# Router rows kept as two f16 halves, and one copy for both operands of an expert slot

## The reference

```python
x = x + y @ wo.T                                   # attention's output added
flat = _rmsnorm(x, ln2_w).reshape(-1, Cx)          # the "rows"
probs = jax.nn.softmax(flat @ router_w.T, axis=-1)
tp, ti = jax.lax.top_k(probs, TOPK)
tp = tp / (jnp.sum(tp, axis=-1, keepdims=True) + 1e-09)
weights = jnp.sum(tp[..., None] * jax.nn.one_hot(ti, NE, dtype=flat.dtype), axis=1)
for e in range(NE):
    hh = jax.nn.silu(flat @ w1[e].T) * (flat @ w3[e].T)
    out = out + weights[:, e:e + 1] * (hh @ w2[e].T)
```

## Time and profile before

| | |
|---|---|
| median of 3 runs | 642.7 us (641.38 to 644.53) |
| the profiled execution, its own time | 643.15 us |
| its span, first to last instruction | 641.2 us |
| mean granted TensorE clock | 0.911 |
| PE / DVE / ACT / POOL busy in the span | 80% / 68% / 49% / 41% |

### The profile page before, as it was taken

One profiled execution on the slowest core, in us unless ns is written; L12 is line 12 of the kernel. 1 busy time (PEld: TensorE's weight loads), 2 busy tenths in 40 slices (PEclk: granted clock), 3 DMA queues, 4 the chain that ended last, 5 costly groups with the idle time before them and its releaser, 6 DMA issues.

```text
span 641.2 us, 12049 instructions
## 1 busy us (share of the span) xinstructions
PE 512.5 (80%) x3865; PEld 285.6 (45%) x3865; DVE 438.4 (68%) x1084; ACT 316.8 (49%) x525; POOL 265.9 (41%) x300
## 2 busy tenths in 40 slices
PE   2999967799998999976767889989665766676891
PEld 2533324577776455433213323235210255466780
DVE  6898948979999556676866978997530157564653
ACT  0778976469996001202254436746522473354550
POOL 3000005035354323033536959992563037743442
PEclk9999996799999999986768999999785999799986
DMA  8999953000158500112233220011143035446775
GB/s 308 394 424 421 371 176 123 10 18 19 33 225 328 129 16 6 40 29 67 57 90 80 68 56 1 1 33 46 57 126 89 20 96 153 126 137 164 209 193 171
DMA packets 45606, 81.92 MB, mean 128 GB/s; under 512 B 8016, under 2 KB 36992, under 8 KB 41200
## 3 DMA queue, kind: packets, MB, share of 16 engines
q1 hardware_dynamic: 41824, 76.33, 36.7%
q0 software_dynamic: 2272, 4.69, 2.1%
q10 hardware_dynamic: 1456, 0.22, 0.2%
HBM read 61.72 MB, written 17.11 MB: 123 GB/s over the span
## 4 chain that ended last, share of the span: by engine, by line
PE 43%; DVE 16%; issue 8%; SPq 5%; DMA 4%; ACT 3%; another core or an unknown queue 3%; POOL 0%; ACTq 0%; DVEq 0%; POOLq 0%
PE ps L1489 8%; DVE A L2306 7%; PE ps L1666 7%; PE ps L1417 6%; PE ps L1400 5%; PE ps L1658 3%; PE ps L1566 3%; PE ps L1769 2%; SPq L770 2%; SPq L767 2%; PE ps L1514 2%; DMA A<-slots_out 2%; PE ps L1792 1%; DMA A<-slots_in 1%
## 5 line engine op out<-in xcount | busy, mean ns | idle before, releaser
L1229 ACT ACTIVATE A<-ps 128x1024 f32<-128x1024 f32 (+3 forms) x80 | 68.6, 894 | 67.1 <-PE ps L1658 47.5
L2306 DVE TENSOR_REDUCE A<-ps 128x1 f32<-128x512 f32 (+3 forms) x160 | 86.1, 603 | 12.9 <-PE ps L1566 12.2
L941 POOL TENSOR_TENSOR G<-G,A 128x1024 f32<-128x1024 f32 (+3 forms) x40 | 73.3, 1874 | 16.5 <-ACT A L1229 16.5
L1658 PE MATMUL ps<-A 97*128 97x512 f16 (+3 forms) x160 | 46.9, 379 | 17.4 <-ACT A L1229 17.4
L1566 PE MATMUL ps<-A 96*128 96x512 f16 (+3 forms) x160 | 54.6, 380 | 7.7 <-DVE A L2306 4.8
L1489 PE MATMUL ps<-A,G 128*128 128x512 f32 x128 | 60.1, 601 | 0.0
L1323 PE MATMUL ps<-R,G 128*128 128x512 f32 x128 | 59.2, 605 | 1.0 <-DVE G L1866 0.8
L1769 PE MATMUL ps<-A 128*128 128x128 f16 (+1 forms) x702 | 50.3, 228 | 7.2 <-issue 7.2
L1417 PE MATMUL ps<-R 128*128 128x128 f16 x768 | 50.4, 224 | 6.9 <-DVE x L1986 4.3
L1417 PEld LDWEIGHTS ps<-R 128*128 128x128 f16 x768 | 47.4, 101 | 14.4 <-issue 5.1
L1092 ACT ACTIVATE R<-ps,b 128x512 f32<-128x512 f32 x64 | 44.0, 687 | 16.0 <-PE ps L1400 9.5
(11 more groups left out here) (309 smaller groups left out, 939.7 us busy)
## 6 DMA issues: line engine op xcount, KB each, us to landing
A<-in_adj_t SPq DMA_DIRECT2D x16, 1024.0 KB, 17.5
A<-w_split SPq DMA_DIRECT2D x39, 341.0 KB
slots_in<-xn SPq DMA_DIRECT2D x1, 8320.0 KB, 22.4
R<-in_adj_in SPq DMA_DIRECT2D x7, 1024.0 KB, 7.2
xn<-in_adj_in SPq DMA_DIRECT2D x5, 1024.0 KB, 12.8
xT<-in_adj_in SPq DMA_DIRECT2D x4, 1024.0 KB, 13.0
A<-in_f_w SPq DMA_DIRECT2D x16, 170.5 KB
w_split<-A SPq DMA_DIRECT2D x8, 341.0 KB, 5.1
```

The costliest lines, as they stand in the source:

```text
L941: pool.tensor_tensor(total, total, probabilities(n, pair)[:, :, t0:CW], ALU.add).then_inc(s_sum, 1)
L1229: act.activation(probabilities(n, pair)[:, :, t0:CW], ps[:, 2 * pair:2 * pair + 2, t0:CW], ACT.Exp, scale=1.0 / (SQ * SQ * float(HD) ** 0. ...
L1658: last = pe.matmul(ps[:, h, t0:CW], keys(j // TPC, h // (NH // NKV))[0:KQ + 1, P * (j % TPC):P * (j % TPC) + P], queries(c, h)[0:KQ + 1, t ...
L2306: dve.reduce_max(pm[:, h, t % TPC, b:b + 1], ps[:, bank, 0:width], AX_X).then_inc(s_rmf, 1)
```

## The change

The rows are kept as two f16 halves of 128 columns in the same 512 bytes of a record. The factor `SX` goes into `rd`, so that the halves are operands as they are. The high half is written as the rows were (ACT for chunk 0, DVE for chunks 1 to 3). The low half is a new DVE operation for each tile, with `xn` and the high half as inputs; for chunk 0 it is a new unit `low_rows` in turn (2, 0). The second copy is now a copy of the first (one ACT operation for a chunk; for chunk 3 POOL as before, in f16). The transposes of a chunk become pairs of f16 products with the identity that add up in the bank, and a slot's transpose becomes two f16 products, side by side; ACT copies both at once as 256 columns, and `slot_low` on DVE is gone. What waited for DVE's low half (`s_sxl`) waits for ACT's copy (`s_sxh`).

```diff
-                       (1, 7): [("rows", 0)], (2, 1): [("tr", 0)], (2, 2): [("rows2", 0)], (2, 3): [("logit", 0)],
+                       (1, 7): [("rows", 0)], (2, 0): [("low_rows", 0)], (2, 1): [("tr", 0)], (2, 2): [("rows2", 0)], (2, 3): [("logit", 0)],
...
-            chain(pool.tensor_copy(second_rows[:, TILES[2], 0:D], first_rows[:, TILES[2], 0:D]))
+            chain(pool.tensor_copy(row_halves[1][:, TILES[2], 0:2 * D], row_halves[0][:, TILES[2], 0:2 * D]))
...
-            def router_rows(c, which):
+            def high_rows(c):
 
                 act.wait_ge(s_r2, c + 1)
...
-                    last = act.activation(row_of(which, t)[:, 0:D], xn[:, t, :], ACT.Copy, scale=rd[:, t:t + 1])
-                last.then_inc(s_fn2 if which else s_fn, 1)
+                    last = act.activation(row_halves[0][:, t, 0:D], xn[:, t, :], ACT.Copy, scale=rd[:, t:t + 1])
+                last.then_inc(s_rhi, 1)
+
+            def copy_rows(c):
+
+                act.wait_ge(s_fn, c + 1)
+                act.activation(row_halves[1][:, TPC * c:TPC * c + TPC, 0:2 * D], row_halves[0][:, TPC * c:TPC * c + TPC, 0:2 * D],
+                               ACT.Copy).then_inc(s_fn2, 1)
...
-                act.activation(x16[2 * (n % 2)], ps[:, x_bank(n), 0:P], ACT.Copy, scale=SX).then_inc(s_sxh, 1)
+                act.activation(x_pair[n % 2], ps[:, x_bank(n), 0:2 * P], ACT.Copy).then_inc(s_sxh, 1)
...
-                        last = pe.transpose(ps[:, bank, P * q:P * q + P], first_rows[:, TPC * c + q, 0:D], ident[:, :])
+                        for part in range(2):
+                            last = pe.matmul(ps[:, bank, P * q:P * q + P], row_halves[0][:, TPC * c + q, D * part:D * part + D],
+                                             ident_h[:, :], start=part == 0, stop=part == 1, skip_group_check=True)
...
-                pe.transpose(ps[:, x_bank(n), 0:P], slot_rows(n)[:, 0:D], ident[:, :]).then_inc(s_sT, 1)
+                for part in range(2):
+                    last = pe.matmul(ps[:, x_bank(n), P * part:P * part + P], slot_halves(n)[:, D * part:D * part + D], ident_h[:, :],
+                                     start=True, stop=True, skip_group_check=True)
+                last.then_inc(s_sT, 1)
...
+                if c == 0:
+                    dve.wait_ge(s_rhi, 1)
+                else:
+                    dve.wait_ge(s_r2, c + 1)
+                    for t in tiles:
+                        last = dve.tensor_scalar(row_halves[0][:, t, 0:D], xn[:, t, :], rd[:, t:t + 1], None, ALU.mult)
+                    chain(last)
+                for t in tiles:
+                    last = dve.scalar_tensor_tensor(out=row_halves[0][:, t, D:2 * D], in0=xn[:, t, :], scalar=rd[:, t:t + 1],
+                                                    in1=row_halves[0][:, t, 0:D], op0=ALU.mult, op1=ALU.subtract)
                 last.then_inc(s_fn, 1)
...
-                dve.scalar_tensor_tensor(out=x16[2 * (n % 2) + 1], in0=ps[:, x_bank(n), 0:P], scalar=SX, in1=x16[2 * (n % 2)],
-                                         op0=ALU.mult, op1=ALU.subtract).then_inc(s_sxl, 1)
```

More of the change, by code:

```diff
@@ L254, in program @@
         second_rows = R[:, NT * RW:2 * NT * RW].rearrange("p (t w) -> p t w", w=RW)
+        row_halves = [rows.rearrange("p t w -> p (t w)").bitcast(F16).rearrange("p (t w) -> p t w", w=2 * RW)
+                      for rows in (first_rows, second_rows)]
         ROWS_AT = 2 * NT * RW + 10 * NT * 8
@@ L271, in slot_rows, with slot_halves @@
             return homes[n]
+        x_pair = [A16[:, 13, 6 * CW + 2 * P * n:6 * CW + 2 * P * n + 2 * P] for n in range(2)]
+        def slot_halves(n):
+            return slot_rows(n)[:, 0:D].bitcast(F16)
         def loaded_target(n):
@@ L2332, in unit @@
                     row_statistics(what[1])
-                elif what[0] == "rows" and what[1]:
+                elif what[0] == "rows" and what[1] or what[0] == "low_rows":
                     router_rows(what[1])
@@ L2396, in router_rows @@
             def router_rows(c):
-                dve.wait_ge(s_r2, c + 1)
-                for t in range(TPC * c, TPC * c + TPC):
-                    last = dve.tensor_scalar(first_rows[:, t, 0:D], xn[:, t, :], rd[:, t:t + 1], None, ALU.mult)
+                tiles = range(TPC * c, TPC * c + TPC)
+                if c == 0:
[8 more added lines that the diff above has]
+                                                    in1=row_halves[0][:, t, 0:D], op0=ALU.mult, op1=ALU.subtract)
                 last.then_inc(s_fn, 1)
```

32 lines of the change are left out of this document (15 added, 17 removed).

## The result

The changed kernel takes 649.63 us (median of 6 runs, 647.51 to 652.17); the kernel before, on the same chip, 642.9 us. The ratio is 1.0099, with a 95% interval of 1.0062 to 1.0136: slower by more than 0.5%. The time lies 1.1 us from the forecast of 648.5 and within its range; the experiments will show that its terms were further off than that, in both directions.

What follows compares the result with a forecast made beforehand. Bound: chunk 2 without slack on PE, DVE and POOL, and SP's queue in the last 22 slots. Terms -0.4 + 0.4 + 0.9 + 4.9 = +5.8 us on 643.15 gave 649.0, forecast as 648.5 us; range 643.0 to 651.0.

Steps and rivals of the forecast that it cites:

- `low_rows` in turn (2, 0): Chunk 2: DVE's four low halves are held until POOL's block of adds runs dry, making PE late: +4.9 us.
- rival 1: Chunk 2: DVE slips in between two of POOL's adds; 643.9 to 646.4 us in all, chance 0.35.
- POOL's lateness: Chunk 2: POOL's seventh add starts 5.2 us late, but with some 3.2 us in hand it does not bind.
- Rows of chunks 1 and 2: Chunk 3, before the first scatter: eight more DVE operations start the scatter 1.85 us later; +0.9 us, between 0 and 1.85.
- Rows of chunk 3: Chunk 3's rows: four added DVE low halves (0.95), less shorter PE products (0.2) and an earlier split (0.3): net +0.4 us.
- The slots: Slots: DVE loses 11.1 us of low halves, but SP sets the late pace, so only -0.4 us (-1.0 to +0.1).
- the faster cases: Whole kernel: slots pay, or some of PE's holes in chunk 3 vanish; faster by over 0.5%, chance 0.10.
- The 1.26 us: Chunk 2: length of the one POOL add running when DVE arrives, taken as a share of the largest add's 2.38.
- Rival 2: Late slots: SP is not the bound and 22 slots gain 0.28 us each, 6.2 us; 642 to 638 us, chance 0.06.
- Rival 3: Chunk 3: holes during the scatters grow with the shift, 1.85 us or more stays; 651 us and over, chance 0.07.
- Rival 4: Slots: halves emptied by more operations than before; ruled out by the order of operations, no chance given.
- The other signs: Changed profile: PE waiting 390 to 396, POOL idle at 394, last maximum 431, scatter 1.9 us later, loads 10 us apart.

Runs made afterwards that it cites:

- e1_low_rows_earlier: Changed kernel with the first chunk's four low halves moved from turn (2, 0) to turn (1, 7): 613.68 us against 610.38 for the kernel before, ratio 1.0051.
- c_after: Changed kernel timed once more, without an edit, on the same chip as c_before: 652.8 us, ratio 1.014 to the kernel before.
- e5_odd_width: Changed kernel with turn (2, 0) as a four-column memset and four one-SBUF-input operations over 127 columns: 652.15 us against 644.07 for the kernel before, ratio 1.014.
- e2_one_input: Changed kernel with the four operations in turn (2, 0) reading one SBUF input in place of two: 621.51 us, ratio 1.0176 to the kernel before.
- the first experiment: The run e1_low_rows_earlier: changed kernel with the first chunk's low halves in turn (1, 7), 613.68 us, ratio 1.0051 to the kernel before.
- e4: Kernel before with DVE's high halves of the rows of chunks 1 and 2 computed twice, eight more operations: 611.0 us, ratio 1.0006 to the kernel before.
- c_before: Kernel before timed once more, without an edit, on the same chip as c_after: 641.53 us, ratio 0.9982.
- e6_slots_undone: Changed kernel with low halves in turn (1, 7) and the slots' part undone: 642.09 us against 644.07 for the kernel before, ratio 0.9992.
- e3: Kernel before without DVE's 39 low halves of the slots: 609.45 us against 610.38 for the kernel before, ratio 0.9976.
- e7: Changed kernel with four memsets of 128 columns in turn (2, 0) in place of the low halves: 612.43 us against 609.96 for the kernel before, ratio 1.0027.
- e1_again: Changed kernel with low halves in turn (1, 7), timed again on the fourth chip: 614.45 us against 609.96 for the kernel before, ratio 1.0069.

## Why the prediction was right, and where it was not

**`low_rows` in turn (2, 0), +4.9 us.** This was said to be the term that decides, and it is: with the low halves (or operations that wait as they do) in that turn the kernel is at 1.010 to 1.018 of the kernel before, without them at 1.003 to 1.007. Its size was too small: the stage is 6.4 to 7.4 us longer in four traces. Two steps of it failed.

First, how DVE waits. I had it held until POOL's block runs dry, then the four in a row. It is let in once at the end of each addition. By the prediction's own sign (the first of the four takes some 5 us, or under 0.5 for rival 1) the 0.46 us measured pointed at rival 1. But rival 1 priced a single catch with the four behind it at +0.3 us; here each of the four pays for an addition of its own. The total happened to be alike, and that is luck: additions of 1.3 to 1.85 us, less the part of the first that had run, against a block of 5 us. PE goes on at 396.55, 5.2 us late if the 1.28 us by which the chunk started later are taken off 390.07, where 5.9 were expected.

The product at the chunk's end shows that the pattern of the prediction exists too. It is held to the end of POOL's block in the earlier trace rows, and for 2.63 us above; in the 14 traces it takes 2.0 to 3.2 us. The slots have a harder case, in e1_low_rows_earlier: DVE's low half (0.56 us by itself) is held through all four of POOL's additions of L964, and PE stands 4.71 us behind it.

```profile
523.31 4.92 POOL L964 TENSOR_TENSOR x<-x,xn 128x512 f32<-128x512 f32 x4
523.39 5.27 DVE L2474 TENSOR_TENSOR A<-A 128x384 f16<-128x384 f32 x1 [0.59 <-ACT A L1282]
528.81 0.40 PE L1809 MATMUL ps<-A 128*128 x2 [4.71 <-DVE A L2474]
```

It takes 5.0 to 5.3 us in all eight traces of the chips with short holes, of either kernel, so it is not the change's doing. What sets the two patterns apart at these places of the program: `add_to_sums` has two semaphore waits ahead of each addition; the four of L964 have none, and those of the chunk's end at most one. No run tested whether that is what decides.

Second, what follows the wait. I counted PE late by 5.9 us and took off 1 us for its idle time in the rest of the chunk. Instead the stage grew by more than PE's wait. PE came out of the idle time at clock 0.50, in a stage where it is busy for 39.7 of 42.7 us, and the sum had no term for the clock. The four traces had stretches of different length at 0.50, and the rest of the loss goes with them (us; late and longer are against a trace with the twelve maxima in a row):

```
run            PE late   then at 0.50 for   stage longer   less PE late
c_after          5.2            3.4              6.4             1.3
after            5.2            5.2              6.9             1.7
e5_odd_width     5.0            5.3              6.8             1.8
e2_one_input     5.0            6.4              7.4             2.4
```

So of the 7.4 us between e2 and e1 some 5.0 are PE's wait and 2.4 the clock, and rival B of the first experiment (the clock costs most) is out by this reading. No run took the clock away alone, so this split is read from the traces and not from an experiment.

POOL's lateness did not bind, as said, though it is larger than the 5.2 us of the prediction: its seventh addition starts 6.4 us late, and L928 at 434.38 is as late. The stage is later still (6.9), and between 396 and 434 us no wait of PE, DVE or ACT is ended by POOL.

**Rows of chunks 1 and 2, +0.9 us (0 to 1.85).** The first scatter is 2.4 us later than the maxima's end gives (23.39 for 21.00), where 1.85 was counted; the four low halves cost 1.14 us and not 0.9. What of it reaches the end is 0.5 us where the holes are short (54.95 for 54.40) and 0.0 in e4. The bounds held where the holes are short; on the other two chips, where chunk 3 is shorter by 2 to 7.5 us, the term can't be read.

**Rows of chunk 3, +0.4 us.** From POOL's last root to PE's transposes, in the earlier trace rows and here, DVE's part grows from 0.88 to 2.05 us; PE starts 2.20 us behind the high halves' start (521.51 less 519.31) and not 1.02, so 1.2 us more. The term had the 1.14 us of the low halves at 0.95. It took 0.3 us off for an earlier split, and that came: DVE's split starts 0.74 us behind the last transpose (523.26 here), where it was 1.04. It took 0.2 off for shorter products, and of that next to nothing came: the eight f16 products take 0.61 us in c_after at full clock, for 0.63 of the four f32 ones. Here they take 1.01 at half clock. c_before's four f32 transposes at the same place and half clock take 1.09, so the clock there is not the change's doing. From the high halves' start to the split it is 0.8 us more, at full clock (c_after against before) and at half (after against c_before).

```profile
516.35 0.88 DVE L2400 TENSOR_SCALAR R<-xn,rd 128x128 f32<-128x128 f32 x4 [1.16 <-POOL rd L951]
...
517.37 1.09 PE L1592 MATMUL ps<-ident,R 128*128 128x128 f32 x4 [1.19 <-DVE R L2400]
```

The stage `front` differs by 3.9 us in the first pair, but half of that is this clock: PE's 16 f32 products ahead of it took 1.13 us for eight in the trace of before, and 2.0 in those of after and of c_before. Against c_before it is 1.3 to 1.7 us in after, e5 and c_after, but 1.3 less in e6_slots_undone, which has the four low halves too. On the short-hole chips nothing is to be seen (51.9 and 53.4 without the low halves, 52.0 to 54.3 with them).

**The slots, -0.4 us.** That the gain on DVE is worth next to nothing held: 0.9976 with all of it and nothing paid. The reason given, that SP alone sets the pace, holds by half: PE's products of two slots are in the chain as well, in the earlier trace rows and in e3, and DVE is not. From SP's load of slot 17 to the end it is 76.05 and 76.06 us in the first pair, as forecast. Whether the part costs 1 to 3 us elsewhere is open, as told above.

**What the sum owed to chance.** By the traces the terms are rather +6.9 (chunk 2), +0.8 to +1.3 (rows), and 0 to +3 (late slots), which is 8 to 11 us; the measured 1.0099 and 1.014 are 6.4 and 9.0 us. In the first pair of traces 7.5 us vanished in chunk 3's holes. The prediction had left room for this with the faster cases ("some may vanish") and put nothing of it into the sum. The error of 1.1 us is a difference of larger errors: with the ratio 1.014 of the third chip the same kernel would have come to 651.7 us, beyond the range's 651.0. And of the 0.3 to 0.7% that remain on the short-hole chips with no wait in chunk 2 only some 1.3 us are accounted for.

**A sum.** The 1.26 us that the prediction calls a share of 2.38 is what an addition of 512 columns takes; the share would be 1.19. Nothing rests on the difference.

**The rivals.** Rival 1, DVE slips in between: half right in its mechanism (it does get in between two additions), wrong in its price, since it does so four times. Rival 2, the slots pay: out, by e3. Rival 3, the holes grow with the shift: not seen on any of the four chips; chunk 3 is shorter, or longer by no more than 0.5 us. Rival 4 was out by the order.

**The other signs.** PE waits from 391.5 to 396.55 (390 to 396 forecast), POOL has its first idle time at 395.7 (394), the chunk's last maximum is at 434.3 (431), the first scatter starts 2.4 us later than that gives (1.9), and SP's record loads are 9.7 to 10.5 us apart (10, and not under 9.5).

**A version to keep?** Moving the low halves to the turn before mends the loss in chunk 2 (1.0051 and 1.0069 in place of 1.010 to 1.018), but nothing tried beats the kernel before by more than the noise. e3 bounds what taking the low halves off DVE could bring if it were free: 0.24%, at most 0.5%.

## What to carry to other kernels

Before putting DVE work into a stage where POOL runs back to back, ask of each operation whether it reads SBUF alone (two inputs there, or a `tensor_scalar` from SBUF to SBUF): beside `add_to_sums` such ones were let in one per POOL operation, so their price was their number times POOL's duration and not their own; beside the blocks without two waits between the operations a single one waited for the whole block (up to 5.3 us). Here 1.14 us of work in DVE's idle time, with POOL idle, cost chunk 2 nothing, where the same work beside POOL's additions cost it 6.4 and 6.9 us. And where a wait stops PE for some us, add PE's next stretch at the lower clock to the price: by the table above 1.3 to 2.4 us here, on top of 5.

## What the runs showed of the hardware

The forms beside POOL's additions, all at the same place: `scalar_tensor_tensor` with two SBUF inputs 5.35 us for four (1.14 with POOL idle); `tensor_scalar` from SBUF f32 to SBUF f16 5.13 for four; memset 0.34 for four, undelayed; maxima over PSUM 0.68 each, undelayed; in e7 the split of the transposes (L2358, one input in PSUM and one in SBUF) 0.69, undelayed. A reduction from SBUF to SBUF (L2328, 0.22 us, at 435.00 above) passes beside POOL's L928 too. I had expected only the first form to wait.

```profile
388.77 0.69 DVE L2355 CAST xT<-ps 128x512 f16<-128x512 f32 x1
389.50 0.69 DVE L2358 TENSOR_TENSOR xT<-ps,xT 128x512 f16<-128x512 f32 x1
```

Chunk 3 takes 73 to 81 us on two of the chips and 54 to 55 on the other two, with the same program. The difference stands in a few long waits ("holes") of ACT and PE while POOL issues its scatters. In before, c_before and c_after the largest are, on ACT:

```profile
491.26 1.94 ACT L1229 ACTIVATE A<-ps 128x1024 f32<-128x1024 f32 x2 [12.10 <-remote]
...
488.64 1.94 ACT L1229 ACTIVATE A<-ps 128x1024 f32<-128x1024 f32 x2 [13.49 <-remote]
...
494.39 1.94 ACT L1241 ACTIVATE A<-ps 128x1024 f32<-128x1024 f32 x2 [18.76 <-remote]
```

"remote" means that the profile shows nothing that ended the wait. In c_after PE had made the scores for this exponential by 476.9 and then stood for 16.71 us behind it; the profile names nothing that ACT waited for. In e1_again ACT has no wait of this kind in the whole stage, and none of its exponentials of full width stands idle for more than 1.8 us behind the one before. What ACT waits for there is open; no run was aimed at it. For whoever times this kernel it means that a change of 1% must be timed beside the kernel before on the same chip, and that chunk 3 can differ by several us between two versions for reasons that lie outside the change.
